# Query and key expansions of attention and retention on 32 rows each, in pairs; another order and another bank in retention

## The reference

```python
x = x + 0.5 * ffn(layernorm(x))
x = x + retention(layernorm(x))
x = x + 0.5 * ffn(layernorm(x))
```

```python
q, k = rotary(q), rotary(k)
r = einsum("bhtd,bhsd->bhts", q, k) * dk ** -0.5 * decay_mask   # causal
out = einsum("bhts,bhsv->bhtv", r, v)
y = (silu(x @ W_g) * group_norm(out)) @ W_proj
```

## Time and profile before

| | |
|---|---|
| median of 3 runs (lowest, highest) | 1073.31 us (1070.42, 1078.86) |
| the profiled execution | 1071.67 us, of which 1069.9 is the span from first to last instruction |
| busy share of the span | TensorE 83%, VectorE 71%, ScalarE 64%, GpSimd 58% |
| mean granted clock of TensorE | 0.936 of full speed |

### The profile page before, as it was taken

How to read it: one execution, slowest core, us unless ns; L and a number is a source line. 1 busy time by engine, 2 the same in 40 slices (tenths; PEclk the granted TensorE clock), 3 DMA queues, 4 the chain that set the end, 5 groups by cost and what they waited for, 6 DMA issues and landing times. The chain is left out here.

```text
span 1069.9 us, 26869 instructions
## 1 busy us (share of the span) xinstructions
PE 891.4 (83%) x8603; PEld 662.6 (62%) x8603; DVE 761.7 (71%) x1900; ACT 687.3 (64%) x1402; POOL 618.9 (58%) x913
## 2 busy tenths in 40 slices
PE   5898999999957883788888888799999999975884
PEld 4566666666636883566666665666666666644884
DVE  4687888888864874465555655578888888873776
ACT  2586888888835772344343434488888888853764
POOL 4144657566572774366657666426575665652666
PEclk9898999999988996799999999799999999996998
DMA  9984991000017773000000000000000000006772
GB/s 307 411 328 56 367 405 45 10 20 10 21 36 216 245 221 94 1 1 1 0 0 0 0 0 1 1 2 12 11 20 10 20 15 15 22 20 195 213 215 89
DMA packets 41958, 97.70 MB, mean 91 GB/s; under 512 B 5240, under 2 KB 25486, under 8 KB 37276
## 3 DMA queue, kind: packets, MB, share of 16 engines
q1 hardware_dynamic: 36380, 84.16, 23.9%
q0 software_dynamic: 5504, 12.63, 3.3%
HBM read 44.68 MB, written 53.13 MB: 91 GB/s over the span
## 5 line engine op out<-in xcount | busy, mean ns | idle before, releaser
L1251 DVE TENSOR_REDUCE mx<-duo 128x4 fp32r<-128x1024 f32 x256 | 312.4, 1220 | 74.3 <-PE duo L540 69.4
L970 ACT ACTIVATE probs<-duo 128x1024 f32<-128x1024 f32 x256 | 263.2, 1029 | 54.1 <-PE duo L546 50.6
L540 PE MATMUL duo<-stacks 32*128 32x256 f32 x1024 | 133.7, 338 | 32.9 <-DVE mx L1251 26.8
L596 PE MATMUL duo<-probs,v_st 128*32 128x256 f32 x2048 | 140.9, 394 | 0.9 <-ACT probs L970 0.6
L1473 DVE TENSOR_TENSOR ret<-duo,dm 128x768 f32<-128x768 f32 x64 | 61.2, 957 | 104.2 <-PE duo L785 100.4
L546 PE MATMUL duo<-q_st,stacks 32*128 32x256 f32 x1024 | 131.2, 335 | 0.1
L540 PEld LDWEIGHTS duo<-stacks 32*128 32x128 f32 x1024 | 80.7, 191 | 68.9 <-issue 39.0
L1625 POOL TENSOR_TENSOR a_ln<-mv_ln,eps_ln 128x2 f32<-128x2 f32 x32 | 6.4, 199 | 145.8 <-DVE mv_ln L1216 145.8
L533 PE MATMUL duo<-qk_hi,sel_r 128*128 128x256 f32 x256 | 83.3, 345 | 7.4 <-DVE qk_lo L1240 7.4
L596 PEld LDWEIGHTS duo<-probs,v_st 128*32 128x32 f32 x2048 | 54.3, 111 | 42.2 <-issue 3.4
L546 PEld LDWEIGHTS duo<-q_st,stacks 32*128 32x128 f32 x1024 | 77.8, 188 | 1.4 <-ACT probs L970 0.5
(11 more groups left out here) (213 smaller groups left out, 2423.4 us busy)
## 6 DMA issues: line engine op xcount, KB each, us to landing
x_sorted<-ret SPq DMA_DIRECT2D x2, 17476.0 KB, 52.8
wbuf<-w_pack SPq DMA_DIRECT2D x38, 512.0 KB, 3.4
ret<-x_sorted SPq DMA_DIRECT2D x22, 257.0 KB, 3.5
stacks<-x_sorted SPq DMA_DIRECT2D x12, 257.0 KB, 3.7
wside<-w_pack SPq DMA_DIRECT2D x38, 66.0 KB, 4.0
w_pack<-wbuf SPq DMA_DIRECT2D x2, 1024.0 KB, 7.8
decay_rows<-prow SPq DMA_DIRECT2D x1, 1536.0 KB
probs<-x_sorted SPq DMA_DIRECT2D x4, 257.0 KB, 4.3
```

Source lines behind the costliest of these rows:

```text
L540: return pe.matmul(score_bank[h % 2][:, t * SEQ:(t + 1) * SEQ], q_st[r:r + 32, g, t * P:(t + 1) * P], k_st[r:r + 32, g, :], start=True, st ...
L596: last = pe.matmul(pv_bank[32 * j:32 * j + 32, cols], v_st[:, t, h, :], probs[:, h % RING, t, :], start=(t == 0), stop=(t == TT - 1))
L970: act.activation(probs[:, h % RING:h % RING + 2, :, :], duo_now[:].rearrange("p (n t q) -> p n t q", n=2, t=TT), ACT.Exp, scale=SCALE).the ...
L1251: dve.tensor_reduce(rows, score_duo[:].rearrange("p (n t k) -> p n t k", n=2, t=TT), AX.X, ALU.max, negate=True).then_inc(max_done, 1)
```

## The change

It has three parts.

1. Columns of the key weights are rolled by 32 (in `packed`, with the rotary tables and the selection matrices to match), so that group g of the query lies in rows 32g and up, and group g of the key in the 32 rows behind them. An expansion now takes 32 rows of the selection matrix and of `qk_hi` or `qk_lo`, in two row groups: query and key high, then query and key low. Query goes to one bank and key to another: `bank_a` and `bank_c` in attention, banks 2 and 3 in retention.
2. Since every expansion of attention needs both banks, the other users are dealt out anew (`spread_max` in a and c by turns, `pv_bank` now in the rotation of `take` as "d"), and three things move by a step: `att_to_dims` from step 0 to 1, `position` from 4 to 5, VectorE's `place` from steps 4 and 5 to 5 and 6.
3. In retention, the value products of both halves go to bank 6 (bank 3 for the last batch), and the order changes: expansion 0 of the next batch ahead of scores 3, the second half's value products ahead of expansion 2, scores 2 ahead of the transposes back to tokens, and VectorE's two rotations ahead of the mask of scores 1.

```diff
-                        sel[p, g, kind, 32 * j + HD * part + d] = 1.0
+                        sel[(p + 32 * (kind // 2)) % P, g, kind, 32 * j + HD * part + d] = 1.0
...
+    A["Wk"], A["bk"] = np.roll(A["Wk"], 32, 1), np.roll(A["bk"], 32)
+    A["W_qkv"] = np.concatenate([A["W_qkv"][:, 0:P], np.roll(A["W_qkv"][:, P:2 * P], 32, 1), A["W_qkv"][:, 2 * P:]], 1)
...
+        def value_bank(b):
+            return bank[3] if isinstance(b, int) and b >= BATCH - 1 else bank[6]
...
-                return {"a": bank_a, "b": bank_b, "c": bank_c}[which]
+                return {"a": bank_a, "b": bank_b, "c": bank_c, "d": pv_bank}[which]
...
-                o = take("caac"[g], ex_ready, b * 8 + 2 * g + 2)
-                for n in range(2):
-                    half = o[:, n * SEQ:(n + 1) * SEQ]
-                    pe.matmul(half, sel_r[:, g, 2 * n, :], qk_hi[:, n, :], start=True, stop=False)
-                    last = pe.matmul(half, sel_r[:, g, 2 * n + 1, :], qk_lo[:, n, :], start=False, stop=True)
+                o = take("a", ex_ready, b * 8 + 2 * g + 1), take("c", ex_ready, b * 8 + 2 * g + 2)
+                for m, part in enumerate((qk_hi, qk_lo)):
+                    for n in range(2):
+                        r = 32 * ((g + n) % GROUPS)
+                        last = pe.matmul(o[n][:, 0:SEQ], sel_r[r:r + 32, g, 2 * n + m, :], part[r:r + 32, n, :], start=(m == 0), stop=(m == 1))
...
-                o = take("aaca"[g], q2_ready, b * 4 + g + 1)
+                o = take("acac"[g], q2_ready, b * 4 + g + 1)
...
-                if g == 0:
-                    pe.wait_ge(va_ready, b + 1)
-                    wait(pe, un_ready, b * 2)
-                if g == 2:
-                    pe.wait_ge(vb_ready, b + 1)
-                    pe.wait_ge(un_ready, b * 2 + 1)
+                if g % 2 == 0:
+                    pe.wait_ge((va_ready, vb_ready)[g // 2], b + 1)
+                    take("d", un_ready, b * 2 + g // 2 + 1)
...
-                o = take("ba"[t], att_ready, b * 2 + t + 1)
+                o = take("db"[t], att_ready, b * 2 + t + 1)
...
-                o = take("c", attT_ready, b + 1)
+                o = take("a", attT_ready, b + 1)
...
-                o = take("c", y1_ready, b + 1)
+                o = take("d", y1_ready, b + 1)
...
-                            if live(i - 2, base):
-                                att_to_dims(i - 2)
                         elif p == 1:
                             if live(i - 1, base):
                                 weigh_values(i - 1, 1)
+                            if live(i - 2, base):
+                                att_to_dims(i - 2)
+                            if live(i - 1, base):
                                 spread_max(i - 1, 3)
...
                                 weigh_values(i - 1, 2)
+                        elif p == 5:
                             if live(i - 3, base):
                                 position(i - 3)
-                        elif p == 5:
...
+                    def expand_pair(b, g):
+                        if g == 0:
+                            pe.wait_ge(rlo_ready, b + 1)
+                        wait(pe, rex_ready, b * 4 + g)
+                        for m, part_ in enumerate((qk_hi, qk_lo)):
+                            for n in range(2):
+                                r = 32 * ((g + n) % RGROUPS)
+                                last = pe.matmul(bank[2 + n][:, 0:SEQ], sel2_r[r:r + 32, g, 2 * n + m, :], part_[r:r + 32, n, :],
+                                                 start=(m == 0), stop=(m == 1))
+                        last.then_inc(rex_ps, 1)
+
+                    def weigh(b, quad):
+                        pe.wait_ge(ret_ready, b * 4 + 2 * quad + 2)
+                        pe.wait_ge(vcopy, b * 2 + quad + 1)
+                        into = value_bank(b)
+                        if isinstance(b, int) and b == BATCH - 1 and quad == 0:
+                            pe.wait_ge(rex_ready, 4 * BATCH)
+                        wait(pe, oT_ready, b * 2 + quad)
+                        for j in range(4):
+                            o, h = into[32 * j:32 * j + 32, 0:SEQ], 4 * quad + j
+                            pe.matmul(o, v_use(b, 0, h), ret[:, h, 0:256], start=True, stop=True)
+                        for j in range(4):
+                            o, h = into[32 * j:32 * j + 32, 0:SEQ], 4 * quad + j
+                            last = pe.matmul(o[:, P:2 * P], v_use(b, 1, h), ret[:, h, 256:384], start=False, stop=True,
+                                             skip_group_check=True)
+                        last.then_inc(ro_ps, 1)
+
...
+                        if s == 0:
+                            if live(i, 0):
+                                scores(0)
+                                expand_pair(i, 1)
+                            if live(i + 1, 0):
+                                to_dims(i + 1)
+                        elif s == 1:
+                            if live(i - 1, 0):
+                                weigh(i - 1, 1)
+                            if live(i, 0):
+                                expand_pair(i, 2)
+                            if live(i + 1, 0):
+                                queries_keys(i + 1)
+                            if not late(i) and live(i - 2, 0):
+                                gated_to_dims(i - 2)
+                        elif s == 2:
+                            if live(i, 0):
+                                scores(1)
+                                expand_pair(i, 3)
+                            if live(i + 1, 0):
+                                values(i + 1)
+                        elif s == 3:
+                            if live(i, 0):
+                                scores(2)
+                            if live(i - 1, 0):
+                                out_to_tokens(i - 1)
+                        elif s == 4:
+                            if live(i - 2, 0):
+                                if late(i):
+                                    gated_to_dims(i - 2)
+                                else:
+                                    project(i - 2)
+                        elif s == 5:
+                            if live(i, 0):
+                                weigh(i, 0)
+                            if late(i) and live(i - 2, 0):
+                                project(i - 2)
+                            if live(i + 1, 0):
+                                gates(i + 1)
+                        elif s == 6:
+                            if live(i + 1, 0):
+                                expand_pair(i + 1, 0)
+                            if live(i, 0):
+                                scores(3)
...
-                o = (bank_c, bank_a, bank_a, bank_c)[g]
-                act.activation(q_st[:, g, :], o[:, 0:SEQ], ACT.Copy).then_inc(ex_ready, 1)
-                act.activation(k_st[:, g, :], o[:, SEQ:2 * SEQ], ACT.Identity, bias=ones_col[:]).then_inc(ex_ready, 1)
+                act.activation(q_st[:, g, :], bank_a[:, 0:SEQ], ACT.Copy).then_inc(ex_ready, 1)
+                act.activation(k_st[:, g, :], bank_c[:, 0:SEQ], ACT.Identity, bias=ones_col[:]).then_inc(ex_ready, 1)
...
-                act.activation(q2_st[:, g, :], (bank_a, bank_a, bank_c, bank_a)[g][:, 0:SEQ], ACT.Copy).then_inc(q2_ready, 1)
+                act.activation(q2_st[:, g, :], (bank_a, bank_c)[g % 2][:, 0:SEQ], ACT.Copy).then_inc(q2_ready, 1)
...
+                            act.activation(r_st[:, ge, :, :], duo[1][:].rearrange("p (a t) -> p a t", a=2)[:, :, 0:SEQ], ACT.Copy).then_inc(rex_ready, 1)
...
+                        elif p == 5:
                             if live(i - 3, base):
                                 place(i - 3, base, 0)
-                        elif p == 5:
                             if live(i + 1, base):
                                 split_qk(i + 1)
-                            if live(i - 3, base):
-                                place(i - 3, base, 1)
-                                place(i - 3, base, 2)
                             if live(i + 2, base) and not ahead(i, base):
                                 layer_norm_moments(i + 2, "prep")
                         elif p == 6:
                             if live(i - 1, base):
                                 normalize(i - 1, 0)
+                            if live(i - 3, base):
+                                place(i - 3, base, 1)
+                                place(i - 3, base, 2)
...
+                        if s == 2:
+                            for n in range(2):
+                                if live(i + 1, 0):
+                                    rotate(i + 1, n)
...
-                        if s == 2:
-                            for n in range(2):
-                                if live(i + 1, 0):
-                                    rotate(i + 1, n)
```

195 lines of the change are left out of this document (88 added, 107 removed).

## The result

| kernel | median us | lowest to highest | clock of each run |
|---|---|---|---|
| before | 1074.26 (4 runs) | 1070.42 to 1078.86 | 0.936 in the profiled one |
| changed | 1093.61 (4 runs) | 1088.01 to 1096.75 | 0.892, 0.903, 0.891, 0.901 |

The ratio is 1.0173, 95% interval 1.0108 to 1.0238: slower by over 1%, where 1049 us was forecast. The profiled execution of the changed kernel took 1096.75 us, its span is 1094.9, 25.0 more than the span of before. Stage marks of the two traces split these: up to the first mask of retention +3.0, retention's fifteen intervals from the first mask of one batch to that of the next +1.5 (227.2 to 228.7), the way to the first maximum of the second attention +1.2, from there to its last maximum +9.1, its tail +4.9, the experts behind it +5.3.

What follows compares the result with a forecast made beforehand. TensorE's waits were taken to bound retention; in attention TensorE, VectorE and ScalarE were nearly full. 1071.7 - 23.9 (retention) + 0 (attention) = 1047.8, given as 1049 us for retention's start and end; range 1036 to 1066.

Steps and rivals of the forecast that it cites:

- about six, 10 us, and I keep that cost: Retention: about six batches at a lowered clock cost 10 us before, and the forecast keeps that cost.
- 1.6 us long together in place of 1.33, hardly more: Retention: the two waits around scores 0, about 1.2 and 0.4 us, hardly exceed the old 1.33 us.
- The rival of the clock: Retention: the clock falls in every batch, nine more falls cost 15 us, 1064 us in all; chance 0.13.
- the prediction's own signs of being wrong: Attention's TensorE waits for shift copies, retention's mean clock is below 0.92, or its full-clock batch exceeds 13.5 us.
- The full-clock batch, 12.87 us: Retention: one batch at full clock takes 12.87 us, 1.59 less than 14.46; fifteen intervals save 23.9 us.
- The 0.19 goes: Retention: TensorE's 0.19 us wait for the output add goes, as the mask ahead of it is done earlier.
- the swap of expansion 0 and scores 3 gives nothing: Retention: scores 0 still starts at 1.89 us, as the mask of scores 3 replaces the wait for ScalarE's copy.
- The expansion itself: Both stages: four matmuls take 0.22 us, not 0.48, saving 0.26; each added change of shape costs 0.11.
- about 0: Attention, per batch: -0.12 + 0.18 - 0.09 us, about 0; -0.3 at best, +0.2 at worst.
- `position` in step 5 at +0.18: Attention: the position matmuls, 0.18 us, enter a step whose end shows no wait, so the batch grows 0.18 us.
- TensorE's savings would only lengthen its waits for the maximum: Attention: work saved in step 0 only lengthens step 1's 0.29 us wait for VectorE's maximum, gaining 0.
- The slower rival: Attention: users of bank a form a ring, four expansions per batch wait 0.35 us, +45 us, 1094; chance 0.07.

Runs made afterwards that it cites:

- e5: Kernel before with only the retention part of the change, its expansions on all 128 rows: 1046.88 us, 0.9742.
- e9: Kernel before with only the retention part of the change (32-row expansions), plus two unread 128-row matmuls behind scores 3: 1048.33 us, 0.9738.
- e13: e9 with its two unread matmuls on 32 rows in place of 128: 1064.67 us, 0.9895.
- e12: Kernel before with only the retention part of the change, both rounds of every 32-row retention expansion issued twice: 1072, 1091, 1095 and 1098 us.
- e10: e5 plus two unread matmuls behind scores 3: 1046.57 us, 0.9720.
- e7: Changed kernel with VectorE's last two placing steps back in attention's step 5: 1080.46 us, 1.0056.
- e4: Changed kernel with `position` back in attention's step 4 and `place` back in steps 4 and 5: 1095.06 us, 1.0202.
- e1: Kernel before with only the attention part of the change, retention as before: 1090.74 us, 1.0173.
- e14: Changed kernel with the edit of e7 and retention's expansions on all 128 rows: 1051.51 us, 0.9759.
- e3: Changed kernel with every expansion, in attention too, on all 128 rows: 1054.27 us, 0.9854.
- e11: Kernel before with only VectorE's addition to `counts` moved from attention's step 5 to step 6, behind the first normalisation: 1078.25 us, 0.9993.

## Why the prediction was wrong, step by step

**The step that failed is "about six, 10 us, and I keep that cost", the cost of the clock in retention.** It was kept as it stood before, on the ground that the new waits are "1.6 us long together in place of 1.33, hardly more". The waits were right (1.14 and 0.32 us), and the longer one brings four falls only with full rows (e5). What I left out is what stands between the waits: matmuls on 32 rows hold the clock less well than matmuls on 128, at equal time (e9 against e13) and at equal waits (e5 against e12). The clock falls in every interval of the same order on 32 rows, and in none but the first if two unread matmuls on 128 rows stand in the wait. By the profiled executions the clock costs 228.7 - 15 x 13.20 = 30.7 us in retention; before it cost 227.2 - 15 x 14.46 = 10.3, so that is 20.4 more than was kept. The rival of the clock named falls in every batch, at 15 us and 0.13. It took each at 1.63 us, as before; about half of them are twice as long and cost 3.0. Two of the prediction's own signs of being wrong came: a clock below 0.92 in retention, and a period of attention more than 0.2 us off.

**The full-clock batch, 12.87 us: mechanism right, size off.** It measured 13.20. TensorE, then VectorE, in e9, in a batch at full clock:

```profile
554.12 0.38 PE L797 MATMUL duo<-qk_hi,sel_r 32*128 32x256 f32 x2
...
554.55 0.39 PE L782 MATMUL duo<-stacks 64*128 64x256 f32 x2
...
556.14 0.39 PE L782 MATMUL duo<-stacks 64*128 64x256 f32 x2
...
557.34 0.41 PE L821 MATMUL duo<-small,s_nat 128*128 128x128 f32 x2 [0.32 <-DVE rows L1544]
...
563.31 0.39 PE L782 MATMUL duo<-stacks 64*128 64x256 f32 x2
...
566.26 1.13 PE L870 MATMUL duo<-wg,sT 128*128 128x256 f32 x4 [0.23 <-DVE xs L1564]
```
```profile
565.19 0.69 DVE L1550 TENSOR_REDUCE ssq<-att_pair 128x16 f32<-128x512 f32 x1 [0.34 <-ACT att_pair L1155]
565.79 0.41 DVE L1564 TENSOR_TENSOR xs<-duo,xs 128x256 f32 x1
```

Expansion 0 takes 0.43 us to scores 3, not 0.33; scores 0 starts at E+2.02 (1.89), the transpose at E+3.22 (3.0), scores 2 at E+9.19 (8.9), gates at E+12.14 (11.8). The 0.19 us wait for the output add, which I let go, is still there, at 0.23: the add stands behind the sum of squares, which waits 0.34 us for ScalarE's square of the transposes to tokens, and those had been put behind scores 2. So "The 0.19 goes" is wrong. Fifteen batches at 13.20 give 18.9 us, not 23.9. That the swap of expansion 0 and scores 3 gives nothing held: the mask took the place of the copy, and scores 0 comes 0.13 us later. The expansion itself takes 0.44 us where it is followed by full-height work (558.46 to 558.90 in e9's trace), as forecast. But at full clock 32 rows give only 13.28 - 13.20 = 0.08 us per batch over full rows: the time that they save goes into the wait for the gate's bank, which full rows do not have, and into the wait for the mask of scores 1 (scores 2 starts 1.22 us behind the values in e9, 1.10 in e10). Of the 1.26 us that a batch gained, 1.18 stand on full rows too: they come from order and banks.

**Attention, "about 0": wrong, +0.28 us per batch against a bound of +0.2.** I costed `position` in step 5 at +0.18; with the placing steps back (e7) the interval is 16.87 with `position` still there, so there it cost nothing. What cost was not priced at all: the VectorE steps moved with it, 0.15 us of work that became 0.65 beside GpSimd. I took the move of `place` for neutral and did not look at what GpSimd does in step 6. The Trainium skill, SBUF — State Buffer, Who interferes with whom, says that a VectorE instruction with two SBUF inputs contends with a GpSimd instruction that reads SBUF, and I should have weighed it ahead. The trace agrees for GpSimd's sums of two SBUF tensors, 0.65 us in place of 0.15. It does not for GpSimd's TENSOR_SCALAR, which reads SBUF too: in ten of eleven batches of before, and all eleven of e7, the whole addition lay beside it and took 0.15 us. GpSimd, then VectorE, in e7:

```profile
830.89 1.57 POOL L1687 TENSOR_SCALAR token_bufs<-token_bufs,mv_ln,rstd_ln 128x128 f32<-128x128 f32 x2 [0.18 <-POOL rstd_ln L1680]
```
```profile
832.14 0.15 DVE L1373 TENSOR_TENSOR counts<-counts,masks 128x8 bf16<-128x8 bf16 x1
```

That TensorE's savings would only lengthen its waits for the maximum held (0.70 to 1.53 us per batch).

**The slower rival** had the right sign at 0.07, and its 1094 was met by chance: TensorE waits for a shift copy once, for 0.2 us, in twelve batches of the changed kernel. Its ring through bank a is real, but shows only where `position` is in step 4 (e4, 17.67 us per batch against 17.18).

**The sum again**, on the span of before: 1069.9 - 18.9 (batch at full clock) + 20.4 (clock) + 9 (0.28 to 0.3 us over some thirty batches) = 1080. The profiled execution stands 15 us above that. 10.2 of them are the tail of the second attention and its experts; the tail took 34.2 us at a mean clock of 0.55, in every other kernel 29.3 to 29.7. Its stretch in the changed kernel, then in e7:

```profile
959.90:994.10 34.20, 17.49 (x130) 10.06 (x126) 15.43 (x68) 8.64 (x12) 15.13 (x21) 0.55 0.15 50
```
```profile
951.90:981.30 29.40, 12.18 (x134) 7.33 (x130) 16.10 (x69) 8.36 (x12) 15.80 (x24) 0.79 0.17 58
```

That the change makes this is not shown. What stays open as well is that e1 costs 16 us where the placing steps explain 8 to 9.

**Attention's 32 rows are the likely rest.** Of the sixteen profiled executions five have attention's expansions on 32 rows: the changed kernel, e1, e4, e7 and e14. In each of them the clock falls, in at least one of the two attentions, somewhere between the first maximum of the fifth batch and the last maximum; in the eleven others it never does. One of the eleven is e3, with the changed kernel's order, banks and placing steps on full rows. The second attention from its fifth batch to its last maximum, changed kernel, then e3:

```profile
761.70:960.10 198.40, 177.37 (x2095) 116.25 (x2097) 172.10 (x379) 165.12 (x303) 123.11 (x192) 0.96 0.04 15
```
```profile
728.80:922.30 193.50, 178.09 (x2093) 123.04 (x2092) 172.12 (x379) 164.71 (x303) 121.90 (x189) 1.00 0.04 15
```

By the ratios full rows in both stages are worth 34 us (1.0173 to 0.9854) and in retention alone 27 (0.9991 to 0.9742), which leaves 7 for attention. The interval of such a difference is wider than that, and no run changes attention's rows alone, so this is a reading of the traces and not shown.

## What to carry to other kernels

Where TensorE waits in every batch, making its matmuls smaller is not free even at equal waits: read the granted clock of the stage, and ask on how many rows the work between the waits runs; if the clock is the cost, work on all rows, or unread work inside a wait, may be the cheaper choice. A small VectorE step that reads two SBUF tensors must be placed by what GpSimd does at that moment, not by VectorE's room alone. Price every instruction that a change moves, the eight-number ones too.

## What was not expected of the hardware

- Two unread matmuls per batch on 128 rows, in a wait of 1.14 us, took 31.6 us off retention (229.0 to 197.4) at no cost in the interval; on 32 rows, for the same 400 ns each, they took off 13.4.
- With the same waits in retention, expansions on 128 rows had a mean clock of 0.97 there, and expansions on 32 rows, issued twice and so longer, 0.83.
- An addition of 128x8 numbers took 0.15 us on VectorE beside GpSimd's TENSOR_SCALAR, and in the steady state of the changed kernel 0.54 to 0.66 us beside GpSimd's sum of two SBUF tensors (up to 0.75 in e11).
